# One core, a fused three-block layer: the second attention's steps in another order, a third PSUM bank for its projections, its rotation split differently over the engines, and its W2 product in two halves of rows

## The reference, cut to what matters

```python
B, T, D = 4, 256, 256            # 1024 tokens in all, 8 tiles of 128
x = x + attn_a(layernorm(x))     # 16 heads, softmax attention
x = x + ffn(layernorm(x))        # int8-quantised 256x256 product
x = x + attn_b(layernorm(x))     # the block that is changed
x = x + ffn(layernorm(x))

def attn_b(hs):                  # H=16 heads, DK=DV=128, M=64 slots
    q, k = rope(hs @ Wq.T), rope(hs @ Wk.T)      # x1*cos - x2*sin, x2*cos + x1*sin
    v, g = hs @ Wv.T, hs @ Wg.T
    s = clip(hs @ Ws1.T @ Ws2.T + bs2, -32, 32)  # per head: T x 64
    z = cumlogsumexp(s, over tokens); es = exp(s); enz = exp(-z)
    A  = tril(q @ k.T) * DK**-0.5
    ok = enz * (A @ es)                          # T x 64 per head
    qv = softmax(ok)
    W2 = tril((qv * enz) @ es.T)
    o  = W2 @ v
    return (o * rsqrt(mean(o*o) + 1e-5) * g_norm_weight * silu(g)) @ Wo.T
```

## Time and profile before

| | us |
|---|---|
| median of 3 runs | 910.02 (909.95 to 910.34) |
| the profiled execution's own time | 908.63 |
| its span, first to last instruction | 906.8 |
| PE busy | 812.4 (90% of the span) |
| DVE busy | 631.1 (70%) |
| ACT busy | 483.4 (53%) |
| POOL busy | 290.9 (32%) |

### The profile page before, as it was taken

The page is one execution under the profiler, slowest core; times in us unless marked ns, Lnnn a source line. Parts: engine busy times, 40 slices in busy tenths (PEclk is TensorE's granted clock), DMA queues, the critical chain, the costliest instruction groups (busy, mean ns, idle before and its releaser), DMA issues.

```text
span 906.8 us, 14154 instructions
## 1 busy us (share of the span) xinstructions
PE 812.4 (90%) x4428; PEld 686.0 (76%) x4428; DVE 631.1 (70%) x1500; ACT 483.4 (53%) x1280; POOL 290.9 (32%) x286
## 2 busy tenths in 40 slices
PE   3999999999999947898998998998989989989964
PEld 2788888888888834677887887787778778777852
DVE  6455555545554588787778778787787877876776
ACT  3455555455555425565574664755655665555420
POOL 6111011010110055245345353352452552452321
PEclk9999999999999988999999998998998999989996
DMA  6010010110101001001001001001010010000001
GB/s 227 1 47 28 19 46 0 46 46 0 46 10 60 1 20 40 1 12 47 0 12 46 0 12 47 9 2 46 12 42 4 12 46 0 12 0 0 1 1 47
DMA packets 23653, 23.74 MB, mean 26 GB/s; under 512 B 2369, under 2 KB 23361, under 8 KB 23506
## 3 DMA queue, kind: packets, MB, share of 16 engines
q1 hardware_dynamic: 23634, 23.51, 8.3%
HBM read 22.45 MB, written 1.05 MB: 26 GB/s over the span
## 4 chain that ended last, share of the span: by engine, by line
PE 63%; DVE 14%; issue 8%; POOL 7%; ACT 7%; DMA 1%; ACTq 0%; POOLq 0%; SPq 0%; DVEq 0%
PE ps L1195 13%; PE ps L1389 9%; PE ps L1200 6%; PE ps L1223 5%; PE ps L1302 4%; POOL rot_s L415 4%; PE ps L1450 3%; PE ps L1266 3%; DVE rot L956 3%; DVE xn L776 2%; PE ps L1242 2%; PE ps L1307 2%; PE ps L1401 2%; ACT wv L709 2%; PE ps L1267 2%
## 5 line engine op out<-in xcount | busy, mean ns | idle before, releaser
L1195 PE MATMUL ps<-xT_hi,w_hi 128*128 128x512 f32 x256 | 109.9, 429 | 3.1 <-DVE xT_lo L783 1.9
L356 POOL TENSOR_TENSOR w_lo<-w_raw,w_hi 128x512 fp32r<-128x512 f32 x32 | 40.7, 1284 | 217.4 <-ACT w_hi L500 217.4
L1195 PE MATMUL ps<-xT_hi,w_lo 128*128 128x512 f32 x256 | 101.6, 397 | 0.0
L1195 PE MATMUL ps<-xT_lo,w_hi 128*128 128x512 f32 x256 | 101.0, 394 | 0.0
L415 POOL TENSOR_TENSOR rot_s<-rot_s,const 128x512 f32<-128x512 f32 x64 | 90.4, 1425 | 28.6 <-ACT rot_s L636 28.6
L986 DVE TENSOR_TENSOR wt<-ps,const 128x384 f32<-128x384 f32 x128 | 69.7, 553 | 27.0 <-PE ps L1402 12.9
L956 DVE TENSOR_TENSOR rot<-rot,const 128x512 f32<-128x512 f32 x64 | 61.3, 958 | 29.5 <-ACT rot_s L636 28.8
L544 ACT ACTIVATE wt<-wt,negmax 128x128 f32<-128x128 f32 (+1 forms) x128 | 56.9, 447 | 36.1 <-DVE negmax L852 36.1
L840 DVE TENSOR_TENSOR v<-ps,bv_b 128x256 f32<-128x256 f32 x64 | 27.0, 424 | 59.4 <-PE ps L1200 59.4
L1389 PE MATMUL ps<-wc_hi,xT_hi 128*128 128x512 f32 x128 | 60.4, 472 | 6.5 <-ACT rot_s L636 6.5
L1200 PE MATMUL ps<-wv,xT 128*128 128x256 f32 x256 | 63.1, 380 | 1.0 <-DVE v L840 1.0
(11 more groups left out here) (155 smaller groups left out, 2283.5 us busy)
## 6 DMA issues: line engine op xcount, KB each, us to landing
w_raw<-a_w_q SPq DMA_DIRECT2D x8, 256.0 KB, 3.3
w_raw<-a_w_k SPq DMA_DIRECT2D x8, 256.0 KB, 3.8
wv<-a_w_v SPq DMA_DIRECT2D x8, 256.0 KB, 2.9
wo<-a_w_o SPq DMA_DIRECT2D x8, 256.0 KB, 3.1
w_raw<-b_Wq SPq DMA_DIRECT2D x8, 256.0 KB, 2.6
w_raw<-b_Wk SPq DMA_DIRECT2D x8, 256.0 KB, 3.6
wc<-b_Wv SPq DMA_DIRECT2D x8, 256.0 KB, 3.6
wc<-b_Wg SPq DMA_DIRECT2D x8, 256.0 KB, 3.9
```

Of the source, the lines that this page charges most:

```text
L356: g.tensor_tensor(lo[:, :, :], raw[:, :, :], hi[:, :, :].bitcast(F32), ALU.subtract).then_inc(ph.w_lo, 1)
L1195: ins = mm(PJ[n[0]], w[:, m, c, h * P:(h + 1) * P], x[:, c, cols], start=(t == 0), stop=(t == len(terms) - 1))
```

## The change

- **Order.** The b_ part of all four engines is rewritten, one list for even and one for odd batches. k0 and k1 are both projected in the even batch, on either side of the output product. c0 to c3 and et are in the odd batch.
- **Three projection banks.** `PJ[2]` is PSUM bank 5, which was `X_[1]`. The table `B_BANKS` says which bank a task uses. The transposes of qp go to the second half of `X_[0]`, those of og into `O_` itself.
- **Rotation.** ACT no longer copies to rot; DVE multiplies by the cosines straight from the PSUM bank. The sum is made by POOL (`rope_add`), not by DVE. A projection bank is now free only when both ACT's copies and DVE's product have read it.
- **ok product.** The moving operand is each head's own 64 columns of es, not both heads' 128.
- **W2 product.** One copy of the transpose, `zT`, in place of the padded z0. Head 0 multiplies partitions 0 to 63 of esT and zT, head 1 partitions 64 to 127, in two PSUM banks, issued in turn.

```diff
-B_FILLS = [[0, 1, 2, 3, 4, 5], [6, 7, None, 8, 9, 10]]
+B_BANKS = ((0, 1, 2, 0, 1, 2, 0, 1, 2, 0, 1), (2, 0, 1, 2, 0, 1, 2, 0, 1, 2, 1))
+ROPES = ["q0", "q1", "k0", "k1"]
...
-        PJ = [ps[:, 0, :], ps[:, 1, :]]
+        PJ = [ps[:, 0, :], ps[:, 1, :], ps[:, 5, :]]
...
+        X_ok = X_[0][:, 0:T].rearrange("p (h t m) -> p h t m", h=2, t=2)
+        X_qt = X_[0][:, T:2 * T]
...
+            def rope_add(r1, k, m, half):
+
+                pool.wait_ge(b_rotcos, r1)
+                pool.wait_ge(b_rotmul, r1)
+                g.tensor_tensor((qT, kT)[m][:, k, half * HALF:(half + 1) * HALF], rot[:, k, :], rot_s[:, k, :],
+                                ALU.add).then_inc(b_rope, 1)
+
...
+                    if b % 2 == 0:
...
+                        if b == 2 and not last:
+                            split_tail(b_, i + 1, 2)
+                        if rest:
+                            exp_tail(phase, 1 - b // 2)
+                        rms(x + b)
+                        if rest:
+                            rope_mul(n("q0"), 0, 0)
+                            rope_mul(n("q1"), 0, 1)
+                            rope_add(4 * phase + 1, 0, 0, 1 - b // 2)
+                            rope_add(4 * phase + 2, 1, 0, 1 - b // 2)
+                        if nxt:
+                            slots(x + b + 1, (b + 1) % B)
+                        if rest:
+                            rope_mul(n("k0"), 1, 0)
+                            rope_add(4 * phase + 3, 0, 1, 1 - b // 2)
+                            rope_mul(n("k1"), 1, 1)
+                            rope_add(4 * phase + 4, 1, 1, 1 - b // 2)
...
-                    s.activation(rot[:, k, :], PJ[bank], ACT.Copy)
...
+                        s.activation(zT[:, :], X_qt, ACT.Copy).then_inc(b_z, 1)
...
-                ap = rot[:, k, :].rearrange("p (b t) -> p b t", b=2)
-                d.tensor_tensor(ap, ap, const[:, col:col + T].unsqueeze(1).to_broadcast([P, 2, T]), ALU.mult
-                                ).then_inc(b_rotcos, 1)
+                d.tensor_tensor(rot[:, k, :].rearrange("p (b t) -> p b t", b=2), PJ[n[0]].rearrange("p (b t) -> p b t", b=2),
+                                const[:, col:col + T].unsqueeze(1).to_broadcast([P, 2, T]), ALU.mult).then_inc(b_rotcos, 1)
...
+                    mm(X_ok[:, h, 0, :], wt[:, h, 0:P], es[:, 2 * b, own], start=True, stop=True)
+                    mm(X_ok[:, h, 1, :], wt[:, h, P:T], es[:, 2 * b, own], start=True, stop=False)
+                    ins = mm(X_ok[:, h, 1, :], wt[:, h, T:T + P], es[:, 2 * b + 1, own], start=False, stop=True)
...
+            def b_w2_product(x, b, i):
+
+                pe.wait_ge(b_z, x + b + 1)
+                bank, count = slot_done(i, b // 2, B_TASKS.index("et"))
+                pe.wait_ge(b_.proj_evac[bank], count)
+                t0 = b * T
+                for h in range(2):
+                    own = slice(h * M, (h + 1) * M)
+                    mm(W_[h][:, 0:T], esT[own, t0:t0 + P], zT[own, :], start=True, stop=True)
+                for h in range(2):
+                    own = slice(h * M, (h + 1) * M)
+                    mm(W_[h][:, T:T + P], esT[own, t0 + P:t0 + T], zT[own, P:T], start=True, stop=True
+                       ).then_inc(b_w2_ps, 1)
```

More of the change, by code:

```diff
@@ L614, in _, with b_task @@
             ffn_copy(0, 2)
[L616 to L619 removed]
+            def b_task(i, h, task_j, half, phase):
+                bank, count = slot(i, h, task_j)
+                done, name = slot_ps(i, h, task_j), B_TASKS[task_j]
                 tl = slice(HT * half, HT * (half + 1))
@@ L661, in b_body @@
                     rest = not (last and b >= 2)
[L662 removed]
+                    nxt = not (last and b == B - 1)
                     half = 1 - b // 2
[L664 removed]
                     phase = 2 * i + 1 + b // 2
[L667 to L672 removed]
@@ L1025, in n @@
                     def n(j):
-                        bank, before = task(NB, i, kb + j)
-                        return bank, before, 2 * NB * i + NB + kb + j + 1
-                    if rest and first:
-                        b_clip_s(n(0), phase)
+                        return (*slot(i, 1 + b // 2, j), slot_ps(i, 1 + b // 2, j))
                     if first:
-                        b_gate(task(NB, i, kb - NB + 10), phase - 1, 3, b // 2)
-                    if last and b == 0:
-                        add_group(b_, x, 0)
@@ L1089, in b_body @@
-                    if rest and first:
-                        b_rope_cos(n(4), 0, 1)
-                        b_rope_add(4 * phase + 3, 0, 1, half)
-                    (add_y if last else add_group)(b_, x + b, b)
+                        b_gate(slot(i, b // 2, NB - 1), phase - 1, 3, b // 2)
+                        if rest:
+                            b_clip_s(n(0), phase)
+                        for h in range(2):
+                            b_mask(wt2[:, h, :], W_[h], b_w2_ps, 2 * (x + b) + h + 1, b_w2)
@@ L1421, in b_body @@
                     rest = not (last and b >= 2)
-                    first = b % 2 == 0
-                    half, pair = 1 - b // 2, i + b // 2
-                    kb = NB * (b // 2)
+                    half = 1 - b // 2
                     phase = 2 * i + 1 + b // 2
                     nxt = not (last and b == B - 1)
-                    own_kb = kb - NB
-                    def fill(f):
-                        j = B_FILLS[b % 2][f]
-                        if rest and j is not None:
-                            bank, before = task(NB, i, kb + j)
-                            b_task((bank, before, None), j, pair, half, phase)
@@ L1483, in b_body @@
-                    ins.then_inc(b_ogt_ps, 1)
-                    if last and b == 2:
-                        for bank in range(2):
-                            pe.wait_ge(b_.proj_evac[bank], NB * PAIRS)
-                        ffn_transpose(1, 0)
-                    if last and b == 3:
-                        ffn_product(1, 1)
-                    fill(4)
-                    if rest and not first:
-                        bank, before = task(NB, i, kb + 10)
-                        free(b_, (bank, before, None))
-                        vg_chunk(bank, 3, half, 0)
@@ L1497, in b_body @@
-                    if last:
-                        pe.wait_ge(b_wos, PAIRS)
-                        out_proj(b_, b, wos)
-                    else:
-                        out_group(b_, i, b)
-                    if last and b == 3:
-                        ffn_transpose(1, 2, (ffns[1].y, 1))
-                    if first:
-                        fill(5)
-                    elif rest:
-                        vg_chunk(bank, 3, half, 1)
+                    c3_bank = slot(i, 1 + b // 2, NB - 1)[0]
```

514 lines of the change are left out of this document (299 added, 215 removed).

## The result

The changed kernel takes 844.95 us (median of 4 runs, 841.37 to 846.64) against 910.02: ratio 0.9279, 95% interval 0.9249 to 0.931, 65 us less. The forecast was 858 (839 to 880), its likeliest case's own range 843 to 872.

The account below looks back on a forecast made before the run. PE was taken as the bound, nearly gapless in b=0 halves, with qp waits and slow clock lengthening b=2 halves. Loop -47.5 us, last pair -2.7 and -1.5, together -51.7: 858 us from the 910.02 median, range 839 to 880.

Parts of the forecast that it names:

- its likeliest case: Whole kernel: waits and slow clock go, W2 saves a part; 858 us, own range 843 to 872, chance 0.52.
- The mechanism: Second attention's loop: equal halves of 28 to 29.5 us, clock 1.00, no qp wait over 1 us.
- The row on contention: DVE's og<-ps, one PSUM input: 1.12 us beside busy POOL, 1.13 beside idle; so the cosine product would not be held.
- The ways to qp: Even batch: POOL's queue from the output product takes 9.8 us against PE's 10.8, so qp is 1.0 us early.
- The second way: From the ok product's end through DVE's ok chain to qp: 4.1 us against PE's 4.6, so 0.5 early.
- Rival 4: POOL's sums make qp 1 to 1.5 us late in each even batch, clock not falling: 880 us, chance 0.13.
- 28.97 busy ... plus 0.5 for short waits: PE in a half: 28.97 us busy, less 2 x 0.35 for W2, plus 0.5 for waits at zT and W2's masks: 28.8.
- W2: PE's W2 product in row halves: bounds 0 and -0.67 us, half taken, -0.35 a batch.
- Rival 3: Row halves not side by side, edit useless for PE, or row changes cost: 869, or 875 with 0.2 a batch; chance 0.14.
- The ok product: PE's ok product with half the columns: bounds 0 and -0.72 us, taken as 0 because weight loads looked like its limit.
- rival 2: PE shorter still: W2 saves 0.67 a batch and the ok product something; 836 to 843 us, chance 0.13.
- Prologue and last pair: Ahead of the loop 0; last pair -2.7 and -1.5 us, from W2's masks no longer late and W2's saving.

Follow-up runs that it names:

- run 8: The changed kernel with ACT's copy to rot back and DVE's cosine product read from SBUF: 881.26 us, ratio 0.9707.
- run 9: The kernel before with only the cosine product read from PSUM (no rot copy; two banks, sums on DVE, wc_lo unmoved): 911.57 us, ratio 1.0046.
- Run 1: The kernel before with only POOL's wc_lo product moved to the head of batch b = 2, ahead of es_lo: 883.06 us, ratio 0.9753.
- run 5: The changed kernel with POOL's wc_lo product moved from the head of batch b = 2 to just ahead of qp: 854.35 us, ratio 0.9414.
- run 3: The changed kernel with the W2 product on whole rows and the padded copy z0 again: 865.47 us, ratio 0.9561.
- run 2: The kernel before with only the W2 product in two row halves and one transpose copy zT: 902.66 us, ratio 0.9956.
- run 10: The kernel before with only the ok product cut to 64 columns per head: 907.38 us, ratio 1.0001.

## Why the prediction was right, and where its sum was off

**The mechanism held.** The halves became equal, the clock stays 1.00 throughout the loop, no wait for qp is left, the cosine product takes 0.68 to 0.69 us beside a busy POOL, and W2 takes 0.85 us (I had written 0.9 to 1.1, so a little less than I allowed). The row on contention was the right one to build on: runs 8 and 9 show it from both sides, 1.80 us with two SBUF inputs beside a POOL product and 0.68 with one in PSUM. The Trainium skill ("SBUF — State Buffer", Who interferes with whom) says this of a VectorE instruction with two SBUF inputs beside a GpSimd one that reads SBUF; the runs agree. In every held row here, VectorE's product ends 0.54 to 0.55 us after POOL's: the 1.68 and 2.88 of the earlier trace rows against the earlier trace rows, the 1.80 and 1.26 of run 8, the 2.15 of run 9. That is most of its own 0.69, so it looks stopped rather than slowed. Run 1 shows that the long wait hung on wc_lo's place. Run 9 shows that the PSUM operand alone does not cure it: the next instruction with two SBUF inputs, the sum, is held in its place. The change takes the sum away from there as well.

**The ways to qp.** I had 9.8 us for POOL's and 1.0 of margin; measured 9.9 and 0.85. The second way, 4.1 us from the end of the ok product, is in fact at most 581.92 - 578.22 = 3.7; POOL's own queue, which runs without a gap from 576.01 to qp, ends last. Run 5 confirms how thin this is: 2.4 us more in the queue give 1.35 us of wait. Rival 4 was a matter of less than one more POOL product.

**The sum was 15.5 us too high** (the profiled time was to be 908.63 - 51.7 = 856.9, and is 841.37). The loop was to take 403 and takes 384.1, 18.9 less. In one half, from start to start of PE's groups (b=0 half of before and of after), 30.18 became 27.43, 2.75 less, where I had 1.38:

| | I took | measured |
|---|---|---|
| waits (at k1 0.72, qp's transposes 0.82, output product 0.34, scores 0.09, less 0.11 for zT) | 1.21 - 0.50 = 0.71 | 1.86 |
| W2, two batches | 0.70 | 0.85 |
| ok, two batches | 0 | 0.12 |
| the rest | -0.03 | -0.08 |

The mis-sized term is the first: "PE's 28.97 busy ... plus 0.5 for short waits". The busy time of a window counts an instruction's whole modelled length, also where the next is merely late. k1's projection took 2.08 us from start to the next start in the half of before and 1.36 now, with the same instructions. The four places in the table add up to 1.97 us, where PE's idle time in that half is 1.21. So 28.97 was not the floor of the work: some 0.8 us of it was waiting. And of the 0.5 us of new waits only 0.11 came: c3's copies ahead of zT cost that, the masks of W2 nothing. The start-to-start times of the same groups in stretches without a wait would have given the floor.

**W2** was taken at half of its bound, 0.35 a batch; the step is 0.47 in the even batch and 0.38 in the odd. Rival 3 had two parts. That the edit does nothing for PE is out. That the two heads really run side by side is the likely reading, not a shown one: no run sends both heads through the same 64 rows. Its second part, that the change between whole and half rows costs something, is partly true. In the odd batch the product starts some 0.09 us later than with whole rows (run 3), which is nearly all of the table's -0.08; rival 3 had 0.2 a batch. Behind the slot product no such price is seen: in run 2 the product follows after 0.98 us, with whole rows after 1.02. On the way back the next projection starts 0.31 us behind L1497, with whole rows in run 3 0.36; a small price could hide in that 0.31. "TensorEngine Tiling (Array Packing)", Key Properties, of the Trainium skill says that a change of mode drains the engine; the 0.09 us agrees with it, and is the only cost of that kind that these runs show.

**The ok product** at 0 was nearly right: 0.05 a batch, no more (run 10). The bound of -0.72, on which rival 2 leaned, is out; rival 2's time (836 to 843) was nearly reached for another reason.

**Prologue and last pair** were to give 4.2 us and gave 0.6, within what the start of the loop alone differs by. PE's waits for the masks in the last pair went from 1.71 and 2.20 to

```profile
797.42 0.49 PE L1511 MATMUL ps<-v,wt 128*128 128x128 f32 x2 [1.10 <-DVE wt L1036]
...
813.17 0.49 PE L1511 MATMUL ps<-v,wt 128*128 128x128 f32 x2 [0.34 <-DVE wt L1036]
```

2.47 us less, and the waits for the transpose's copy ahead of W2 are 0.81 and 0.47 us where they were twice 0.86. But PE now waits 2.30 us for ACT's wos in this pair (775.84) and 2.32 for DVE's qb of the FFN behind it (805.79), where the kernel before shows no such wait. The term counted what goes and not what comes in its place. The clock in the tail differs from run to run too. This part I did not take further.

**Where the gain comes from.** The parts do not add up one by one. Undone singly in the changed kernel they cost, in the loop: the PSUM cosine 30.7 (with ACT's copy), the row halves with the single copy 15.4, wc_lo's place 11.7, the third bank 4.2, the sums on POOL 2.5. Done singly in the kernel before they bring: wc_lo's place 28.4, the row halves 1.1 (beside wc_lo), the ok columns 0.05 to 0.08 us an undisturbed half, the PSUM cosine nothing (0.5% slower). The row halves turn into time only in the changed kernel; that its order does this, rather than the rest of the change beside it, is argued and not shown. With wc_lo moved and W2 halved but in the old order, the loop is 421.1; the remaining 37 us to 384.1 come of the order together with the PSUM cosine, the bank, the sums and the ok columns. All of these but the PSUM cosine bring 6.4 us (run 8, 414.77), and the cosine then the other 30.7; taken the other way round the split may differ. How the 37 split between order and cosine stays open: the old order, with wc_lo where it was, can't use the PSUM cosine (run 9), the new one can't do without it (run 8).

## What to carry to other kernels

An engine's list is paid for by what stands beside it as much as by what stands ahead: where VectorE and GpSimd work at once, give VectorE an input in PSUM, or put the GpSimd instruction where VectorE does something else; here moving one POOL instruction (2.85 us in its old place, 2.4 in the new) was worth 4 us in every other half. Then ask what the PSUM operand holds: a bank that a second reader must leave needs that reader early in its list, or PE pays for it (run 9: 0.9 to 1.6 us a time). A saving on the bound engine counts only where its next releaser is early; the same edit was worth 0.1 us in one order and 1.1 in the other. And for the floor of a stage take start-to-start times of groups that waited for nothing, not the busy sum.

## What the runs showed of the hardware

- Two fp32 matmuls on half the rows each (64*128, in two banks, issued in turn): the four instructions of 256 columns take 0.54 us instead of 0.86 on whole rows, the four of 128 columns 0.31 instead of 0.36. The gain is in the wide ones. Ahead of them, behind a whole-row projection, 0.09 us is given back (0.32 for 0.23 to 0.24).
- Twelve fp32 instructions with 64 columns take 1.39 us, with 128 columns 1.44.
- A wait of 1.35 us of PE in each b=2 half leaves the clock at 1.00 (run 5), and so do waits of 0.93 to 1.58 us in every half (run 9). Behind 2.76 us it fell to 0.50. It does not always: of the 21 waits of 2.73 to 2.77 us in the profiles of the kernel before and of runs 2 and 10, the clock stayed at 1.00 behind two.
- A 128x512 VectorE product with two SBUF inputs that starts while a POOL product reads SBUF ends 0.54 to 0.55 us after it, for POOL products of 1.25 to 2.85 us (five rows); alone it takes 0.68 to 0.69.
- wc_lo on POOL takes 2.39 us beside DVE instructions with at most one SBUF input of this size (570.62 above) and 2.84 beside the sum that it holds (run 9): both lose.
